# Turning the first gathered expert tile ahead of the last shared product, in a mixture-of-experts and graph layer on one core

## What is computed

```
flat = layernorm(x) * ln_scale + ln_bias            # 1250 x 512
h_shared = swiglu(flat @ shared_in_w.T)             # 1250 x 1024
out_shared = h_shared @ shared_out_w.T + shared_out_b
h_expert = swiglu(flat @ expert_in_w.T)             # 1250 x 1024, the same for all experts
# a gate picks a group and in it 2 of 4 experts for every node: comb, cnt (1250 x 8)
routed = cnt @ expert_out_bias
for e in range(8):
    routed += comb[:, e:e+1] * (h_expert @ expert_out_weight[e].T)
x = x + out_shared + routed
```

## Time and profile before

| what | us |
|---|---|
| median of 3 runs | 738.08 (737.08 to 741.6) |
| the profiled execution, its own time | 737.12 |
| its span, first to last instruction | 735.3 |
| around the span | 1.8 |
| PE busy in the span | 705.9 (96%) |
| DVE, ACT, POOL busy | 386.4, 261.8, 172.8 |

### The profile page before, as it was taken

The page is one execution under the profiler, slowest core; times in us unless marked ns, Lnnn a source line. Parts: engine busy times, 40 slices in busy tenths (PEclk is TensorE's granted clock), DMA queues, the critical chain, the costliest instruction groups (busy, mean ns, idle before and its releaser), DMA issues.

```text
span 735.3 us, 12086 instructions
## 1 busy us (share of the span) xinstructions
PE 705.9 (96%) x4382; PEld 434.2 (59%) x4382; DVE 386.4 (53%) x735; ACT 261.8 (36%) x386; POOL 172.8 (23%) x170
## 2 busy tenths in 40 slices
PE   5979899999999999989999999999899999999998
PEld 5646477775676556655756644446755455555554
DVE  5874578984677666966255512222245524441154
ACT  3853123224732332265353223333336433532000
POOL 3240000000070000022223257742212112212363
PEclk9999899999999999999999999999999999999999
DMA  9200001100031240012234212232166666644675
GB/s 246 103 1 1 1 1 68 49 2 14 15 130 58 73 158 1 0 29 57 87 113 143 57 29 58 59 92 82 30 229 242 246 239 242 228 145 127 198 193 174
DMA packets 24416, 73.90 MB, mean 101 GB/s; under 512 B 7058, under 2 KB 7404, under 8 KB 20273
## 3 DMA queue, kind: packets, MB, share of 16 engines
q1 hardware_dynamic: 8607, 39.74, 16.1%
q0 software_dynamic: 10768, 25.52, 12.0%
q10 hardware_dynamic: 4994, 8.01, 3.0%
HBM read 57.90 MB, written 15.31 MB: 100 GB/s over the span
## 4 chain that ended last, share of the span: by engine, by line
PE 82%; DVE 10%; ACT 4%; issue 3%; DMA 1%; DVEq 0%; POOL 0%; SPq 0%; ACTq 0%; POOLq 0%
PE banks L1352 62%; PE banks L1401 7%; PE banks L1711 3%; PE banks L1389 3%; DVE st L771 1%; PE banks L1582 1%; PE banks L1375 1%; DMA x<-in_x 1%; PE banks L1591 1%; ACT W L437 1%; DVE xn L1163 1%; PE banks L1382 1%; PE banks L1554 1%; PE banks L1416 1%; ACT big L615 1%
## 5 line engine op out<-in xcount | busy, mean ns | idle before, releaser
L1352 PE MATMUL banks<-W,xT 128*125 128x512 f16 (+1 forms) x1392 | 318.8, 383 | 5.8 <-ACT big L471 2.0
L1352 PEld LDWEIGHTS banks<-W,xT 128*125 128x125 f16 (+2 forms) x1392 | 166.2, 122 | 132.9 <-issue 11.2
L1352 PE MATMUL banks<-xT,W 128*128 128x500 f16 (+1 forms) x720 | 128.3, 339 | 1.8 <-DVE xn L1302 1.4
L1352 PEld LDWEIGHTS banks<-xT,W 128*128 128x128 f16 x720 | 69.8, 97 | 58.1 <-DVE xn L1302 1.6
L748 DVE SCALAR_TENSOR_TENSOR W<-stg,W 128x2048 f16<-128x2048 f32 x30 | 68.5, 2304 | 46.6 <-ACT W L437 46.6
L1352 PE MATMUL banks<-W,big 128*125 128x512 f16 x360 | 81.5, 380 | 0.0
L1352 PEld LDWEIGHTS banks<-W,big 128*125 128x125 f16 x360 | 48.3, 136 | 29.2 <-issue 2.3
L368 POOL TENSOR_TENSOR big<-xn,big 125x512 f16<-125x512 f32 x20 | 23.5, 1173 | 174.7 <-ACT big L630 174.7
L379 POOL DMA_INDIRECT xn<-h_rows,tokidx x29 | 33.9, 1169 | 124.4 <-PE banks L1711 108.9
L1322 DVE CAST xT<-banks 128x1024 f32 x22 | 26.9, 1222 | 61.2 <-PE banks L1711 61.2
L437 ACT ACTIVATE W<-stg 128x2048 f16<-128x2048 f32 x30 | 56.3, 1902 | 0.0
(11 more groups left out here) (324 smaller groups left out, 785.9 us busy)
## 6 DMA issues: line engine op xcount, KB each, us to landing
stg<-in_units SPq DMA_DIRECT2D x30, 1024.0 KB
y_rows<-xT ACTq DMA_DIRECT2D x29, 256.0 KB
h_rows<-big POOLq DMA_DIRECT2D x10, 500.0 KB, 3.6
out_x<-x SPq DMA_DIRECT2D x10, 224.0 KB
stg<-in_wqkT SPq DMA_DIRECT2D x2, 1024.0 KB, 11.2
x<-in_x SPq DMA_DIRECT2D x2, 896.0 KB
xn<-h_rows,tokidx POOLq DMA_INDIRECT x29
x<-in_x SPq DMA_DIRECT2D x1, 448.0 KB
```

The costliest lines, as they stand in the source:

```text
L1352: ins = te.matmul(dst, lhs(sl, c), rhs(sr, c), start=(first and c == 0 and k == 0), stop=(last and c == n - 1 and k == 2))
```

## The change

- The first gathered tile gets a place of its own for its transpose, `hgT0`, in `mscr`, that is not over `xT`. Turn 0 moves in PE's list from behind product 23 to in front of it, and so do the two copies: in ACT's and DVE's lists they now stand between the work of product 22 and that of product 23.
- PE's `borders` is cut in two halves, behind product 18 and behind product 20.
- Expert product 0 reads `hgT0`, and waits for `h_f` 23 instead of 24.
- POOL raises `g_rdy` for tiles 0 and 1 after its low halves 21 and 22, and gather 2 stands in front of low half 23.
- POOL's loop over the later gathers is rolled differently: each gather is followed at once by the wait for its own landing, where before the next gather was issued first.

```diff
+        hgT0 = mscr[:, 4096:5120].bitcast(F16).rearrange("p (s j n) -> p s j n", s=2, j=J)
...
+        def half_borders(eng, z):
+
+            four = eng.value_load(etab[0:1, z:z + 1], min_val=0, max_val=PACK ** 4 - 1)
+            return [eng.snap((four // PACK ** k) % PACK + 1, min_val=4 * z + k + 1, max_val=NT - EXP + 4 * z + k + 1) for k in range(4)]
+
         def borders(eng):
...
+            return half_borders(eng, 0) + half_borders(eng, 1)
...
+                    if n in (3 * J - 3, 3 * J - 2):
+                        gathered(n - 3 * J + 3)
+                    if n == 3 * J - 2:
+                        pool.wait_ge(S["turned"], 1)
+                        gather(2)
                     n += 1
-            gathered(0)
-            for i in range(1, NG):
-                if i + 1 < NG:
-                    pool.wait_ge(S["turned"], i)
-                    gather(i + 1)
-                gathered(i)
+            gathered(2)
+            for i in range(2, NG - 1):
+                pool.wait_ge(S["turned"], i)
+                gather(i + 1)
+                gathered(i + 1)
...
+                    if n == 3 * J - 1:
+                        act.wait_ge(S["turned"], 1)
+                        s.activation(hgT0[:, 0], turned[0], ACT.Copy).then_inc(S["hg_h"], 1)
...
-            act.wait_ge(S["turned"], 1)
-            s.activation(hgT[:, 0, 0], turned[0], ACT.Copy).then_inc(S["hg_h"], 1)
...
-            dve.wait_ge(S["turned"], 1)
-            v.tensor_copy(hgT[:, 0, 1], turned[1]).then_inc(S["hg_l"], 1)
+                    if n == 3 * J - 1:
+                        dve.wait_ge(S["turned"], 1)
+                        v.tensor_copy(hgT0[:, 1], turned[1]).then_inc(S["hg_l"], 1)
...
+                    if n in (18, 20):
+                        pe.wait_ge(S["etab_rdy"], 1)
+                        ends += half_borders(pe, (n - 18) // 2)
+                    if n == 3 * J - 2:
+                        pe.wait_ge(S["cntT_ev"], 3)
+                        pe.wait_ge(S["g_rdy"], 1)
+                        turn(lambda o: hg2[:, o:o + 128])
                     n += 1
...
-            pe.wait_ge(S["cntT_ev"], 3)
-            pe.wait_ge(S["g_rdy"], 1)
-            turn(lambda o: hg2[:, o:o + 128])
-            pe.wait_ge(S["etab_rdy"], 1)
-            ends = borders(pe)
...
-            pe.wait_ge(S["h_f"], 3 * J)
-            expert(0, lambda o: slice(o, o + 128), ps[0][:, :])
+            pe.wait_ge(S["h_f"], 3 * J - 1)
+            expert(0, lambda s, c: hgT0[:, s, c, :], ps[0][:, :])
```

More of the change, by code:

```diff
@@ L1690, in _, with turn @@
                 ins.then_inc(S["cntT_mm"], 1)
+            def turn(rows):
+                for s in range(2):
+                    for j in range(J):
+                        ins = te.matmul(turned[s][:, j, :], rows(s * HID + j * 128), ident16[:, :], start=True, stop=True)
+                ins.then_inc(S["turned"], 1)
+            hg2 = mscr[:, 2048:4096].bitcast(F16)
             pe.wait_ge(S["w_rdy"], U_SIN + 4)
+            ends = []
             n = 0
@@ L1704, in _, with expert @@
                     ins.then_inc(S["h_mm"], 1)
-                    n += 1
[L1708 to L1714, removed]
-            hgT2 = xflat[:, 0:2 * ROWW]
-            pe.wait_ge(S["cntT_ev"], 3)
-            pe.wait_ge(S["g_rdy"], 1)
-            turn(lambda o: hg2[:, o:o + 128])
-            pe.wait_ge(S["etab_rdy"], 1)
-            ends = borders(pe)
+                    if n in (18, 20):
[5 more added lines that the diff above has]
+                        turn(lambda o: hg2[:, o:o + 128])
+                    n += 1
+            hgT2 = xflat[:, 0:2 * ROWW]
             total = ends[EXP - 1]
-            def expert(e, cur, bank):
-                split3(bank, lambda s, c: hgT2[:, cur(s * HID + c * 128)], unitv(U_EXP + 2 * e), J, True, True).then_inc(S["me_mm"], 1)
+            def expert(e, lhs, bank):
+                split3(bank, lhs, unitv(U_EXP + 2 * e), J, True, True).then_inc(S["me_mm"], 1)
             pe.wait_ge(S["hg_h"], 1)
@@ L1742, in _ @@
                     bank = pe.snap((i % 2) * 512)
-                    expert(e, lambda o: bass.ds(cur + o, 128), PSflat[:, bass.ds(bank, 512)])
+                    expert(e, lambda s, c: hgT2[:, bass.ds(cur + s * HID + c * 128, 128)], PSflat[:, bass.ds(bank, 512)])
             pe.wait_ge(S["w_rdy"], U_SOUT + 2)
```

## The result

The changed kernel takes 743.26 us as a median of 20 runs (739.28 to 747.17), against 737.07 for the kernel before (733.37 to 741.6, 20 runs on the same chips): a ratio of 1.0087, with a 95% interval from 1.0068 to 1.0105. It is slower by 0.9%, where 735.3 and a small gain had been forecast. The profiled execution took 743.25, with a span of 741.2.

What follows compares the result with a forecast made beforehand. PE was taken to set the end, with the `y_rows` chain 0.9 us behind; 0.9 in hand plus PE's 4.3 less the tail's 3.0 gave a 2.2 gain, from 737.5 to 735.3 us, range 732.6 to 738.3.

Steps and rivals of the forecast that it cites:

- PE's saving: At the stage's start, turn 0, turn 1 and expert product 0 take 7.11 us instead of 11.43, saving 4.3.
- the list of what to look for: Profile signs: no idle before turn 0, product 23 or turn 1; clock 1.00 from 526 to 536; turn 2 at about 532.7.
- I take no cost, with 3.9 us to spare: In POOL's loop, serial gathers cost nothing: worst long gather plus a quiet one takes 13.4 us, against 17.3 allowed.
- The fourth rival: The loop stalls: two 9.3 us gathers in a row exceed 17.3 by 1.3, about five times; 741.8 us, chance 0.04.
- from expert tile to expert tile without a stop: In the middle of the stage PE never waits: 0.89 us for a turn and 5.18 for a product.
- The tail, 3.0 us: After the last token tile, serial gathers 27 and 28 lengthen the tail by 3.0 us, bounds 1.9 to 4.0.
- Rival 3: In the tail, gathers 27 and 28 keep 8.1 and 6.1 us: tail grows by 8.1, end at 740.4, chance 0.09.
- Gather 2's place: On POOL before low half 23, gather 2 lands at 529.4, before turn 2 asks at 532.7: free.
- The `y_rows` chain's length: At the end, the chain of `y_rows` gathers and additions keeps its length, from 689.72 to 730.91.

Runs made afterwards that it cites:

- e1_overlap: The changed kernel with POOL's old order, each next gather issued before the wait for the one ahead: 732.98 us against 735.84 for the kernel before, ratio 0.9962.
- e2_roll_only: The kernel before with only the new serial roll of POOL's gather loop: 747.14 us, ratio 1.0147.
- e9_quarter_loads: The changed kernel, serial gathers kept, fetching only 512 of 2048 columns of expert weight units 16 to 27: 732.7 us, ratio 0.995.
- e10_reg_turn: The kernel before with turn 1's row address from a register whose value the program can't know ahead: 741.43 us, run once.
- e4_serial_tail: The changed kernel with gathers overlapped up to gather 26 and only gathers 27 and 28 serial: 735.74 us, ratio 0.9992.
- e6_gather2_late: e1_overlap with gather 2 put back behind POOL's low half 23: 735.4 us against 736.21 for the kernel before, ratio 0.9992.
- e7_borders_whole: e1_overlap with the loop bounds loaded in one piece, behind turn 0 and in front of product 23: 733.79 us, ratio 0.9972.
- e3_serial_loop: The changed kernel with gathers serial up to gather 24 and overlapped from gather 25: 741.7 us, ratio 1.0072.
- e8_reg_turn: The kernel before with turn 1's row address from a register whose value is known from its bounds: 737.35 us, run once.

## Why the prediction was wrong

- **PE's saving, 4.3 us: right.** 4.45 between the two profiles. Turn 0, the copies of tile 0, the early gather and the halves of `borders` all found their cover, and the clock stayed at 1.00, as in the list of what to look for.
- **The step that failed: "I take no cost, with 3.9 us to spare", in the loop.** The mechanism was seen and the length too (9.3 us there, 9.31 for gather 4 here). It was held against a deadline, two gathers in a row against 17.3 us. But a serial chain has a rate, and what counts is the mean of latency plus handover against the period of its consumer: 7.5 against 6.07 while weights load. Long and short gathers took turns here, so no two long ones in a row were needed: a long one of 9.31 + 0.77 uses up 4.0 us of lead, and a short one gives back 0.4 (4.87 + 0.77) to 1.2 (4.14 + 0.77), until PE waits. The deadline also took gather 4 as issued on time, and in a serial chain it was not: 25.55 us after product 18, against 23.66 in e1_overlap. e2_roll_only shows this with the roll alone (+10.1 in the loop), e1_overlap takes it away, e9_quarter_loads takes the loads away. The fourth rival came nearest, as a long gather twice in a row, with a chance of 0.04 and 6.5 us for 8.4.
- **What a late tile costs was not priced at all.** Beside the idle time, the turn that waited takes 1.15 more, as its addresses come from registers (e10_reg_turn), and the product behind it may run at half clock, another 1.5. At turn 6 that is 1.16 + 1.15 + 1.49 = 3.8 us for a wait of 1.16. The kernel before had such turns too, so "from expert tile to expert tile without a stop" doesn't hold for its whole loop: turns 9 and 10 took more than 2 us each, and 2.8 us were lost there. Turn 9 came just behind ACT's copy of tile 8, which a store had held up and which ended at 580.04:

```profile
580.35 2.27 PE L1711 MATMUL banks<-ident,xn 128*128 128x128 f16 x16
...
587.91 2.16 PE L1711 MATMUL banks<-ident,xn 128*128 128x128 f16 x16
```

- **The tail, 3.0 us: a term mis-sized.** It is 4.0, at the upper bound that was given. The gathers took 6.4, 4.4 and 4.1 from issue to landing in the chain that ended last, gather 27 less than the 5.1 assumed; but each handover is 0.75 and not 0.3, and gather 26 itself was issued 0.7 later behind the output's first matmul (1.43 against 0.72), being held by the landing of gather 25. Rival 3 was wrong in its 8.1. The tail alone would have left the time inside the range: e4_serial_tail, which has just that, took 735.74.
- **Gather 2's place, "Free": wrong as a statement, right in the sum.** Without its place in front of the low half turn 3 is 2.2 us late (e6_gather2_late). The prediction priced only that it had time to land, not what it would be without it.
- **The `y_rows` chain's length: right, in part by luck.** 41.66 from its first gather to the end of its last addition, against 41.19. In the other profiles it is from 40.2 (e7_borders_whole) to 42.7 (e3_serial_loop), so an agreement within half a microsecond says little.

The 4.45 is not all a typical gain. In the profile of the kernel before the clock fell after the two waits, but in e2_roll_only and e8_reg_turn, whose fronts wait just as long, it stayed at 1.00:

```profile
528.00:530.00 2.00, 0.64 (x12) 0.49 (x10) 1.22 (x1) 1.02 (x1) 0.99 (x2) 1.00 0.00 0
530.00:532.00 2.00, 2.00 (x22) 1.41 (x23) 0.96 (x1) 0.96 (x2) 0.00 (x0) 1.00 0.68 184
```

(e2_roll_only.) There turn 1 takes 1.05 and the front 25.53, so the saving is 3.2 in such executions and 4.45 in the others. e1_overlap's 2.9 has an interval from 1.0 to 4.5 and is in line with either; how often each happens wasn't measured.

## What to carry to other kernels

Where a loop waits for a transfer before it issues the next, compare the mean latency plus the handover with the consumer's period, over the stretch with the most other traffic; a check of one deadline says nothing of a rate. Do the same for every other transfer that a consumer waits for, here ACT's stores. Issue the next transfer before waiting for the last one, even if both buffers look early, and look at what else a re-rolled loop does in its last rounds. When a step is moved ahead, the rest of the edit needs the same accounting: here the moved turn earned 0.4% and a reordering of two lines in another engine's loop cost 1.3%.

## What the hardware showed unexpectedly

- Matmuls with addresses from registers are no slower in a full queue (1.06 for 16), but take 0.14 us each when their wait is satisfied late, 2.15 to 2.27 in all, against 1.05 with fixed addresses.
- After the same pair of idle times of 1.5 and 1.4 us the granted clock fell to 0.50 in one execution and stayed at 1.00 in two others; after 1.16 (changed kernel) and after 1.51 and 1.69 (e10_reg_turn), with a slow turn behind the last wait, it fell to 0.50. After a single wait with a slow turn behind it, it stayed at 1.00 once (0.84, changed kernel) and fell once (0.96, e2_roll_only).
- From the landing of a gather to the issue of the next, with nothing else in POOL's way, 0.77 us pass.
- The issue of a gather takes POOL 0.94 us, and 1.9 to 3.05 where it fell together with DVE's conversion of a weight unit (549.93, 609.21 and 644.26 in the changed kernel).
